# Cross-attention opening: a key chunk's bounce and four extra-row copies moved behind the landing of the first stacks

## The reference, cut to what matters

```python
q   = heads(x @ W_q);  k_t = heads(text @ W_k);  v_t = heads(text @ W_v)
probs_t  = softmax(q @ k_t.T * Dh**-0.5)
text_out = probs_t @ v_t
k_ip, v_ip = heads(ip @ W_k_ip), heads(ip @ W_v_ip)
sem   = l2norm(probs_t @ text) @ l2norm(ip).T
fused = q @ k_ip.T * Dh**-0.5 + 0.5 * sem
ip_out = (softmax(fused) * mask) @ v_ip
out   = (text_out + ip_out) @ W_out + b_out + x
```

## Time and profile before

| what | value |
|---|---|
| device time, median of 3 runs | 729.2 us (726.13 to 729.36) |
| the profiled execution's own time | 730.1 us |
| its span | 728.3 us |
| PE busy | 714.9 us, 98% of the span |
| ACT / DVE / POOL busy | 560.7 / 633.2 / 441.3 us |
| mean granted TensorE clock | 0.995 |

### The profile page before, as it was taken

The page is one execution under the profiler, slowest core; times in us unless marked ns, Lnnn a source line. Parts: engine busy times, 40 slices in busy tenths (PEclk is TensorE's granted clock), DMA queues, the critical chain, the costliest instruction groups (busy, mean ns, idle before and its releaser), DMA issues.

```text
span 728.3 us, 22685 instructions
## 1 busy us (share of the span) xinstructions
PE 714.9 (98%) x7260; PEld 566.1 (78%) x7260; DVE 633.2 (87%) x1879; ACT 560.7 (77%) x1611; POOL 441.3 (61%) x563
## 2 busy tenths in 40 slices
PE   8899999999999999999999999999999999999997
PEld 6677778787887878878787887878788787788764
DVE  5478898989889898998989899898988989899986
ACT  5377787787878878787887878788787877878783
POOL 6435657566565656656566665656666565666684
PEclk9899999999999999999999999999999999999999
DMA  7775664352625435272542636345262543417001
GB/s 246 149 172 121 144 110 114 54 112 72 139 75 88 115 50 116 75 143 68 91 120 42 124 73 122 89 66 122 58 130 77 107 98 59 106 25 139 15 1 21
DMA packets 135355, 70.13 MB, mean 96 GB/s; under 512 B 75352, under 2 KB 134792, under 8 KB 135240
## 3 DMA queue, kind: packets, MB, share of 16 engines
q1 hardware_dynamic: 130856, 65.60, 42.2%
q10 hardware_dynamic: 4064, 2.73, 1.4%
q0 software_dynamic: 320, 0.36, 0.3%
HBM read 41.94 MB, written 15.24 MB: 79 GB/s over the span
## 4 chain that ended last, share of the span: by engine, by line
PE 91%; DMA 3%; DVE 2%; POOL 2%; issue 1%; ACT 0%; SPq 0%; POOLq 0%; ACTq 0%; DVEq 0%
PE ps_gram L888 18%; PE ps_prep L771 18%; PE ps_pT L871 12%; PE ps_gram L889 12%; PE ps_score L858 6%; PE ps_prep L832 5%; PE ps_val L897 4%; PE ps_val L898 2%; PE ps_prep L829 1%; PE ps_prep L802 1%; PE ps_prep L804 1%; DMA w_raw<-in_L_xattn_W_k_ip 1%; PE ps_prep L944 1%; DMA q_st<-q_bounce 1%; POOL dual L624 1%
## 5 line engine op out<-in xcount | busy, mean ns | idle before, releaser
L624 POOL TENSOR_TENSOR dual<-prob 128x371 f32<-128x371 f32 (+1 forms) x288 | 251.3, 873 | 257.9 <-ACT prob L1165 257.7
L888 PE MATMUL ps_gram<-gram_hi,pT_hi 125*128 125x371 f16 (+1 forms) x864 | 273.1, 321 | 2.1 <-DVE pT_lo L1385 1.7
L889 PE MATMUL ps_gram<-gram_lo,pT_hi 125*128 125x371 f16 (+2 forms) x864 | 230.6, 267 | 0.0
L1159 ACT ACTIVATE pT_hi<-ps_pT 125x384 f16<-125x384 f32 (+1 forms) x279 | 134.7, 483 | 108.4 <-PE ps_pT L871 99.1
L1149 ACT ACTIVATE prob<-ps_score,low 128x371 f32<-128x371 f32 (+1 forms) x288 | 165.4, 574 | 26.9 <-DVE low L1380 21.6
L1385 DVE TENSOR_TENSOR pT_lo<-ps_pT,pT_hi 125x384 f16<-125x384 f32 (+1 forms) x279 | 150.2, 538 | 29.7 <-ACT pT_hi L1159 25.4
L1380 DVE TENSOR_REDUCE low<-ps_score 128x1 f32<-128x371 f32 (+1 forms) x288 | 154.7, 538 | 18.5 <-PE ps_score L858 14.2
L1398 DVE CUSTOM_DVE_ANT_0 quad_junk<-ps_gram,dual 128x371 f32<-128x371 f32 (+1 forms) x288 | 152.9, 531 | 6.0 <-POOL dual L624 1.9
L897 PE MATMUL ps_val<-val,pT_hi 125*128 125x84 f16 (+3 forms) x864 | 152.3, 196 | 0.0
L1165 ACT ACTIVATE prob<-prob 128x371 f16<-128x371 f32 (+1 forms) x288 | 151.2, 525 | 0.1
L898 PE MATMUL ps_val<-val,pT_lo 125*128 125x42 f16 (+3 forms) x864 | 141.1, 181 | 0.0
(11 more groups left out here) (280 smaller groups left out, 1520.4 us busy)
## 6 DMA issues: line engine op xcount, KB each, us to landing
ctx_sb<-in_ctx_t SPq DMA_DIRECT2D x15, 750.0 KB, 4.8
w_raw<-k_bounce SPq DMA_DIRECT2D x32, 216.0 KB, 4.0
k_st<-k_bounce SPq DMA_DIRECT2D x28, 216.0 KB, 4.0
k_bounce<-k_hi SPq DMA_DIRECT2D x15, 288.0 KB, 4.2
k_bounce<-k_lo SPq DMA_DIRECT2D x15, 288.0 KB, 4.3
q_st<-q_bounce SPq DMA_DIRECT2D x60, 63.0 KB, 2.4
xt_sb<-in_x_t SPq DMA_DIRECT2D x16, 168.0 KB, 5.5
w_raw<-k_hi SPq DMA_DIRECT2D x32, 84.0 KB, 3.0
```

What stands on the lines that cost most here:

```text
L624: nc.gpsimd.tensor_tensor(dual[0:r, t % 2, :], prob[0:r, g % 4, 0:TX], prob_16[0:r, t % 2, :], ALU.subtract).then_inc(s_dual, 1)
L888: nc.tensor.matmul(ps_gram[t % 2][:, 0:TX], hi, gh[0:TROWS[i], i, :], start=(i == 0), stop=False, skip_group_check=True)
L889: last = nc.tensor.matmul(ps_gram[t % 2][:, i * TC:TX], hi, gl[0:TROWS[i], i, i * TC:TX], start=False, stop=(i == NT - 1), skip_group_chec ...
```

## The change

SyncE waits for the twelve DMAs of `s_first` before it bounces key chunks 1 and 2. GpSimd waits for the same twelve before its four `stack_k_extra`. TensorE issues 4 identity transposes ahead of the first scores and not 28.

```diff
-WARM_UP, STAY_WARM, WAIT_WARM, EXP_WARM = 9, 16, 28, 8
+WARM_UP, STAY_WARM, WAIT_WARM, EXP_WARM = 9, 16, 4, 8
...
             bring_k(start, s_first, 0, XP, stores=1)
+            sp.wait_ge(s_first, 2 * FIRST - 16 * 4)
             bounce_k(start, PIECES_K[1], 1, CC)
             bring_q_extra(start, 1, s_qst[0])
             bring_k(start, s_kst[0], XP, NB)
...
                     stack_q_extra(pool, start, term, 0, s_pool_q[term])
+            pool.wait_ge(s_first, 2 * FIRST - 16 * 4)
             for term in (0, 2, 1, 3):
                 stack_k_extra(pool, start, term, 1, s_pool_k[term])
             for k in POOL_PIECES:
```

## The result

| | before | changed |
|---|---|---|
| device time, median of 22 runs each | 726.16 us (724.72 to 729.36) | 728.88 us (727.68 to 731.05) |
| ratio, 95% interval | | 1.0031 (1.0022 to 1.0041) |
| profiled execution: own time, span | 730.1, 728.3 | 728.87, 727.1 |

The change makes the kernel 0.31% slower: 2.7 us. That is inside the 0.5% that was called "the same", but the forecast was 724.7 in a range of 722.7 to 728.3, with the other sign. Also, the profiled execution from which the prediction started (730.1) lay 3.9 us above the median of the 22 runs, at the slow end of the kernel's spread. Its profile has a span of 724.6 and is the fairer partner: I call it the twin.

The account below looks back on a forecast made before the run. TensorE, busy 98%, was the bound, held in the opening by the late last Q stack. First exps 3.7 + clock 1.0 - context 0.2 = 4.5 us: 725.6 from the profiled 730.1, median 724.7, range 722.7 to 728.3.

Parts of the forecast that it names:

- The stack's landing: Opening: the last Q stack takes 3.0 us from issue and lands at 28.0, with GpSimd's copies and the bounce away.
- rival (b): Last Q stack: only queue turns hold it, not the copies; lands 0.87 us sooner, at 31.0; 728.3 us; chance 0.14.
- The first `exps`: ScalarE, opening: starts at 29.2 and not 32.86, a gain of 3.7 us.
- GpSimd behind its new wait: GpSimd: copies issued by 30.1, context parts to 31.8, x_lo to 32.7; TensorE needs it at 33.4, covered by 0.7 us.
- The clock: Opening: half clock costs 2.1 us; with TensorE loaded sooner, about half the low stretch goes, 1.0 us back.
- SyncE's list: SyncE behind its wait: batch 2's context issued at 36.3, landing at 43.0; ScalarE stands 1.4 us, mostly absorbed, cost 0.2.
- Rival (c): Gain partly given back: batch 2's context at 45 or x_lo after 33.4; about 2 us off, 726.7; chance 0.17.
- The second key part at tile 7: SyncE's bring_k for tile 7 lands at 37.5, at worst 39.5; needed at 42.9, covered by 5.4 us, at worst 3.4.
- rival (d): Tile 7: the second key part is late, slower than before only if landing after 47.4; 731.2 us; chance 0.04.
- The starting point: Base of the forecast: the profiled execution of 730.1 us, taken as 0.9 above a median of 729.2.

Follow-up runs that it names:

- the twin: The kernel before, run again unchanged for a second profile; 725.72 us, ratio 1.0001, profile span 724.6.
- the run without that stall: The changed kernel with GpSimd's three low parts of batch 1 waiting until VectorE's two are done; 728.26 us, ratio 1.0026.
- the kernel with the further moves: Kernel before, no waits, 4 transposes, GpSimd's copies ahead of x_lo, VectorE's context parts ahead of its minima, batch 2's context loads earlier; 727.58 us, ratio 1.0015.
- the last run: The changed kernel with GpSimd's low parts behind VectorE's and SyncE's four small stack_q_extra ahead of its wait; 723.82 us, ratio 0.9969.

## Why the prediction was wrong

- **The stack's landing: right.** 28.0 was forecast for the first scores, 27.05 measured, 0.8 of it because the issue came at 24.18 and not at 24.97; 3.0 us for the last Q stack, 2.9 measured. That GpSimd's copies are the main part was right too, and rival (b), turns only, fell.
- **The first `exps`: right in its gain.** The first `prob` starts at 28.13 (forecast 29.2), against 31.28 in the twin: 3.2 us. The start from the recorded profile was off: against the twin, whose stack takes 4.9 us, the change could win less than against the earlier trace rows.
- **GpSimd behind its new wait: the step that failed.** The prediction timed the parts well (to 31.8 and 32.7; measured 31.1 and 31.9) and wrote "covered", since it asked only when TensorE needs x_lo. It didn't ask who is slowed while they run. In the twin GpSimd's start at 29.40 and end before VectorE's two `text_lo`, at 31.61 (28.88 and 33.19 in the recorded profile). The change moved VectorE's to 28.46, with the first scores, and kept GpSimd's at 29.39, behind its copies: onto each other. That cost 3.1 us, all of the lead. The trace of before had the sign, in rows that the prediction does not use: a VectorE pair of 1.87 us beside a GpSimd dual that takes 1.08 and not 0.87, and, plainer, one `fprob` of 1.11 us beside two of GpSimd's instructions, where the median of its 16 is 0.30.

```profile
702.12 1.11 DVE L1487 SCALAR_TENSOR_TENSOR fprob<-fexp,mask_sb,fmax 112x80 f32<-112x80 f32 x1
...
64.58 1.87 DVE L1318 SCALAR_TENSOR_TENSOR wo_lo<-wo_sb,wo_hi 128x640 f16<-128x640 f32 x2 [0.78 <-ACT wo_hi L1211]
...
65.03 1.08 POOL L624 TENSOR_TENSOR dual<-prob 128x371 f32<-128x371 f32 x1 [1.26 <-ACT prob L1165]
```

- **The clock: wrong sign.** 1.0 us was to come back. Against the twin, which has no low stretch in its opening, 2.3 us went in the profiled execution, as the run with 30 transposes shows. The price of the half clock itself, 2.1, was near: from `pT_lo` to the scores of tile 4 it takes 4.99 us in the recorded profile and 3.27 in the twin, 1.7 less. The wait for `pT_lo` made the idle time that the prediction saw shrinking; and with 4 transposes alone the clock fell as well. The transposes were costed at nothing on the path, which they are, and not as what keeps the clock.
- **SyncE's list: too small.** The context was forecast to be issued at 36.3 and to cost 0.2. It was issued at 37.91, since the small copies took 1.3 us each and not 0.62. The 0.62 is that of the `bring_k` issues in the earlier trace rows; in the same trace the four small copies run from 27.28 to 30.54, 0.8 each. In the changed kernel the first stall hid this; in the run without that stall it took the whole lead, over 3 us, and with `bring_k` and the context issued 3.3 us sooner the kernel is faster than before, 723.82. Rival (c) named this place with "about 2 off", but counted from a kernel faster than before.
- **The second key part at tile 7, rival (d):** not seen at tile 7. Its stall on ScalarE appeared only where the context had been put ahead of it.
- **The starting point.** The median moved from 729.2 to 726.16 with 22 runs. Even a gain of 4.5 us off the recorded execution would have been much less off the typical one, whose first scores come 1.6 us sooner in the twin. With its clock of 0.995 the recorded profile is like the 17 of 122 executions of this kernel that lie at 0.998 or below.

What stays open: why VectorE's second `text_lo` lost although it is recorded 0.47 us ahead of GpSimd's, where a start of 0.31 us ahead wins later in the kernel; how the loss divides in the executions with a clock of 0.998; how the costs of the late SyncE list divide between the second key part and the context; and what slows most executions of the kernel with the further moves.

## What to carry to other kernels

When an edit moves work in time, lay the moved instructions of every engine side by side with what runs then on the others: in this kernel GpSimd's computing on SBUF could stop a VectorE instruction with two SBUF inputs (0.55 us became 4.2), and the profile showed that as a long busy instruction, not as a wait. A lead won at the start is only kept if the next limit moves too, so read the issue list of the engine that is made to wait down to the first transfer that somebody later stands for. Before a forecast of half a per cent, take the median of many executions and compare the profile with it; here one profile in the tail moved the base by 3.9 us, as much as the effect.

## What was not expected of the hardware

- One VectorE instruction of 0.55 us was held through up to four back-to-back GpSimd instructions: 4.2 us in the changed kernel, and 4.79 us for a pair with GpSimd's wait alone. In 27 other meetings of one profile it kept its 0.55 and GpSimd's took up to 0.99 for 0.88.
- SyncE's issue of small SBUF to SBUF copies takes 0.6 us each alone and about 1.3 on average beside GpSimd's four copies (5.16 us for four in the changed kernel, 2.45 with nothing beside them).
- Identity transposes kept the granted clock up ahead of a late stack: without 24 of them, with 2.88 us of idle time ahead of the first scores, none of 12 executions had a mean above 0.998, with them 33 of 35 had 0.999 or more. In the last run, with 4 of them and 0.89 us of idle time, 11 of 12 had 0.999 or more. In the changed kernel the window 32:33 shows 1.00 with 30 of them in the gap and 0.76 with 8, with 1.44 and 3.99 us of idle time behind them.
